# Attention's third score chunk directly behind the other two, in the projection banks; the slot projection in the first chunk's bank

## The reference

```python
def attn(x):                                  # 16 heads, 64 key dims, 64 slots, 128 value dims
    q, k, v = heads(x @ Wq), heads(x @ Wk), heads(x @ Wv)
    s = clip(heads(x @ Ws), -32, 32)          # slot scores
    z = cumlogsumexp(s, axis=time)
    g, p = exp(z_before - z), exp(s - z)
    # recurrence over time:  hk = hk * g + k p^T ;  ok = q . hk      (b h 64 slots)
    pv = softmax(ok)
    # recurrence over time:  hv = hv * g + p v^T ;  o = pv . hv
    o = o * rsqrt(mean(o^2) + EPS) * g_norm_weight * silu(x @ Wg)
    return o.reshape(...) @ Wo
x = layernorm(x + attn(x))
x = layernorm(x + cross_attention(q=x, k=ctx, v=ctx))   # 32 query heads over 8 key heads, 16 dims each
x = layernorm(x + ((silu((x @ gate_w.T) * gate_s) * ((x @ up_w.T) * up_s)) @ down_w.T) * down_s)
```

## Time and profile before

| | us |
|---|---|
| median of 3 runs | 2073.99 (2073.62 to 2078.05) |
| profiled execution | 2075.78 |
| its span | 2074.1 |
| TensorE busy | 2001.5 (97%) |
| VectorE busy | 1378.5 (66%) |
| ScalarE busy | 779.9 (38%) |
| GpSimd busy | 527.1 (25%) |
| mean granted clock of TensorE | 0.99 |

### The profile page before, as it was taken

How to read it: one execution, slowest core, us unless ns; L and a number is a source line. 1 busy time by engine, 2 the same in 40 slices (tenths; PEclk the granted TensorE clock), 3 DMA queues, 4 the chain that set the end, 5 groups by cost and what they waited for, 6 DMA issues and landing times. The chain is left out here.

```text
span 2074.1 us, 30680 instructions
## 1 busy us (share of the span) xinstructions
PE 2001.5 (97%) x11828; PEld 1436.9 (69%) x11828; DVE 1378.5 (66%) x2219; ACT 779.9 (38%) x1918; POOL 527.1 (25%) x575
## 2 busy tenths in 40 slices
PE   7999999999999999999999989999999799999997
PEld 6787877878778777787877753343433378787775
DVE  4666666566666666666666679999999265555556
ACT  2332232322323223232232326888888621211111
POOL 2142151141242143142241253222221011111111
PEclk9999999999999999999999998999999999999999
DMA  4000100001001001001000000111110100000002
GB/s 162 1 1 11 36 1 17 31 11 36 1 11 36 1 11 37 1 11 36 1 11 3 6 14 18 25 27 30 25 25 13 32 16 15 30 15 30 15 16 81
DMA packets 58609, 46.89 MB, mean 23 GB/s; under 512 B 14448, under 2 KB 47216, under 8 KB 58480
## 3 DMA queue, kind: packets, MB, share of 16 engines
q1 hardware_dynamic: 58480, 45.11, 7.3%
HBM read 32.78 MB, written 4.19 MB: 18 GB/s over the span
## 5 line engine op out<-in xcount | busy, mean ns | idle before, releaser
L1268 DVE TENSOR_REDUCE a_raw_qks<-a_ps 128x1 f32<-128x512 f32 x512 | 323.4, 684 | 20.8 <-PE a_ps L694 18.4
L1245 ACT ACTIVATE x_prob<-a_ps 128x512 f32<-128x512 f32 x512 | 279.3, 606 | 68.7 <-PE a_ps L716 67.7
L65 PE MATMUL a_ps<-a_vg_hi,a_xT_lo 128*128 128x512 f32 x512 | 209.6, 409 | 1.1 <-DVE a_vg_lo L1293 1.1
L66 PE MATMUL a_ps<-a_vg_lo,a_xT_hi 128*128 128x512 f32 x512 | 200.4, 391 | 0.0
L67 PE MATMUL a_ps<-a_vg_hi,a_xT_hi 128*128 128x512 f32 x512 | 199.9, 390 | 0.0
L65 PE MATMUL a_ps<-a_xT_hi,a_qks_lo 128*128 128x512 f32 x384 | 157.9, 411 | 1.9 <-DVE a_xT_lo L1299 1.9
L1320 DVE SCALAR_TENSOR_TENSOR a_gate<-a_gate,a_ps 128x256 f32<-128x256 f32 x128 | 52.0, 407 | 152.1 <-ACT a_gate L1136 152.1
L66 PE MATMUL a_ps<-a_xT_lo,a_qks_hi 128*128 128x512 f32 x384 | 150.7, 392 | 0.0
L67 PE MATMUL a_ps<-a_xT_hi,a_qks_hi 128*128 128x512 f32 x384 | 150.7, 392 | 0.0
L694 PE MATMUL a_ps<-a_xT_lo,a_xT_hi 64*128 64x512 f32 x384 | 144.7, 464 | 5.8 <-DVE a_raw_qks L1268 4.2
L579 POOL TENSOR_TENSOR a_f<-a_rs 128x8 f32<-128x8 f32 x32 | 6.5, 203 | 560.7 <-ACT a_flat L1164 560.7
(11 more groups left out here) (180 smaller groups left out, 4578.8 us busy)
## 6 DMA issues: line engine op xcount, KB each, us to landing
a_raw_vg<-in_L_attn_Wv_dram SPq DMA_DIRECT2D x8, 512.0 KB, 4.3
a_raw_vg<-in_L_attn_Wg_dram SPq DMA_DIRECT2D x8, 512.0 KB, 6.7
a_raw_qks<-in_L_attn_Wo_dram SPq DMA_DIRECT2D x8, 512.0 KB, 3.6
a_xT_lo<-a_xT_lo SPq DMA_DIRECT2D x32, 128.0 KB, 2.4
out_dram<-acc SPq DMA_DIRECT2D x8, 512.0 KB, 3.2
x_values<-acc SPq DMA_DIRECT2D x13, 256.0 KB, 2.7
acc<-in_x_dram SPq DMA_DIRECT2D x3, 1024.0 KB, 10.4
f_raw_down<-in_L_ffn_down_w_dram SPq DMA_DIRECT2D x11, 256.0 KB, 2.9
```

What stands on the lines that cost most here:

```text
L65: pe.matmul(out, w_lo, x_hi, start=start, stop=False)
L66: pe.matmul(out, w_hi, x_lo, start=False, stop=False)
L1245: nc.scalar.activation(prob[par][:, s % 4, :], score_bank(q, s, par), ACT.Exp, scale=X_SCALE).then_inc(exp_done[par], 1)
L1268: nc.vector.tensor_reduce(nm[:, q % 2, i % 4, par, i // 4:i // 4 + 1], max_bank(u, q, i, par), AX.X, ALU.max, negate=True).then_inc(max_re ...
```

## The change

In every step but the last, chunk 2 goes into the two projection banks, directly behind chunks 0 and 1, with no wait. S comes behind it, into `ch[0]` (for m > 0), and waits for ScalarE's copy of chunk 0 (`chunk_act` 2m - 1 = 2n + 1). VG follows S directly. It waits for VectorE to have masked head 0 of chunk 2, VG + 1 for head 1. In the last step chunk 2 stays in `ch` with its waits.

In the last step the diagonals go ahead of the first output tile, a second tile moves behind the values, and VectorE's split of the right operand goes ahead of `low_oT`; its additions move with the tiles. In the cross attention VectorE's `normalise` at s = 3 and s = 13 goes ahead of that slice's reductions.

```diff
--- before.py
+++ after.py
@@ -332,6 +332,14 @@
         EARLY = 6
         IN_VALUES = 10
 
+        def slot_bank(m, b):
+
+            return ch[0] if m else pj[b % 2]
+
+        def last_chunk_banks(n):
+
+            return ch if n == NSTEP - 1 else [pj[n % 2], pj[(n + 1) % 2]]
+
         def value_banks(n):
 
             return (okb, tb) if n == NSTEP - 1 else ob
@@ -760,16 +768,20 @@
 
             def project(m, i, b, pair):
 
-                bank = pj[(b + i) % 2]
+                bank = slot_bank(m, b) if i == S else pj[(b + i) % 2]
 
                 if i == S:
-                    wait(pe, right_ready, 2 * m - 1)
+                    wait(pe, chunk_act, 2 * m - 1)
                     pe.wait_ge(s_ready, pair + 1)
                 elif i == VG:
-                    wait(pe, left_ready, 2 * m - 1)
+                    if m:
+                        pe.wait_ge(chunk_dve, 4 * m - 1)
                     pe.wait_ge(vg_ready, pair + 1)
                 elif i == VG + 1:
-                    pe.wait_ge(clip_done, m + 1)
+                    if m:
+                        pe.wait_ge(chunk_dve, 4 * m)
+                    else:
+                        pe.wait_ge(clip_done, 1)
                 else:
                     pe.wait_ge(gate_ready, 4 * m + i - 2)
                 if i == Q:
@@ -809,10 +821,11 @@
 
             def last_chunk(n):
 
-                pe.wait_ge(chunk_act, 2 * n + 1)
-                pe.wait_ge(chunk_dve, 4 * n + 1)
+                if n == NSTEP - 1:
+                    pe.wait_ge(chunk_act, 2 * n + 1)
+                    pe.wait_ge(chunk_dve, 4 * n + 1)
                 for i, col, first in CHUNKS[2]:
-                    mm = blocks(ch, i, col, first, T)
+                    mm = blocks(last_chunk_banks(n), i, col, first, T)
                 mm.then_inc(chunk_done, 1)
 
             def diagonals(n):
@@ -894,9 +907,8 @@
                 pe.wait_ge(e_ready, n + 1)
                 into = n == NSTEP - 2
                 chunks(n)
-                next_project(S)
                 last_chunk(n)
-                next_project(VG)
+                next_project(S, VG)
                 slots(n)
                 states(n, j)
                 if not first:
@@ -975,14 +987,13 @@
                 transpose4(okb, [pv[:, 2 * t:2 * t + 2, :].rearrange("p h m -> p (h m)") for t in range(TT)])\
                     .then_inc(pvT_done, 1)
                 max_pair(0, 7)
-                project_out(n, PAIRS - 1, (0,))
                 pe.wait_ge(left_ready, 2 * n + 2)
                 pe.wait_ge(right_ready, 2 * n + 2)
                 diagonals(n)
-                project_out(n, PAIRS - 1, (1,))
+                project_out(n, PAIRS - 1, (0,))
                 max_pair(0, 8)
                 values(n, B - 1)
-                project_out(n, PAIRS - 1, (2, 3))
+                project_out(n, PAIRS - 1, (1, 2, 3))
                 for i in range(TILES):
                     max_pair(0, 9 + i)
                     if i > 1:
@@ -1312,7 +1323,7 @@
 
             def clip(m, b):
                 dve.wait_ge(proj_done, PROJ * m + 1)
-                nc.vector.tensor_scalar(eT[:, :], pj[b % 2], CLAMP, -CLAMP, ALU.min, ALU.max).then_inc(clip_done, 1)
+                nc.vector.tensor_scalar(eT[:, :], slot_bank(m, b), CLAMP, -CLAMP, ALU.min, ALU.max).then_inc(clip_done, 1)
 
             def gating(m, i, b):
 
@@ -1417,7 +1428,7 @@
                 norm_now = at(p, PAIRS - 1) and j > 0
                 into = n == NSTEP - 2
                 mask_chunks(n, ((0, 1, ch[1]), (1, 1, tb)))
-                mask_chunks(n, ((2, 0, ch[0]), (2, 1, ch[1])))
+                mask_chunks(n, ((2, 0, last_chunk_banks(n)[0]), (2, 1, last_chunk_banks(n)[1])))
                 low_left(eT[:, :], 2 * n + 1)
                 dve.wait_ge(left_ready, 2 * n + 2)
                 clip(n + 1, b1)
@@ -1480,14 +1491,14 @@
                 reduce_max(0, 0, 6)
                 slot_sum(n)
                 scaled_weights(n)
+                low_right(wT, 2 * n + 1)
                 low_oT(n)
-                low_right(wT, 2 * n + 1)
                 reduce_max(0, 0, 7)
                 mask_diagonal_blocks(n)
-                add_out(n, B - 2, (0, 1))
                 reduce_max(0, 0, 8)
+                add_out(n, B - 2, (0,))
                 gated_output(n, B - 1)
-                add_out(n, B - 2, (2, 3))
+                add_out(n, B - 2, (1, 2, 3))
                 for i in range(9, 14):
                     reduce_max(0, 0, i)
 
@@ -1531,11 +1542,13 @@
                                 dve.wait_ge(x_added, 2 * u)
                         if stats_unit and s == 14:
                             dve.wait_ge(norm.stats_ready, norm_of[2] + 1)
+                        if s == 3 and not (first and q == 0):
+                            normalise(u - 1, 1)
+                        if s == 13:
+                            normalise(u, 0)
                         for ahead, i in max_turns(first, q, s):
                             if not (last and q + ahead > 3):
                                 reduce_max(u + ahead, (q + ahead) % 4, i)
-                        if s == 3 and not (first and q == 0):
-                            normalise(u - 1, 1)
                         if s == 4 and not (first and q == 0):
                             add(u - 1, b if q else b - 1, (q - 1) % 4, 1)
                         if stats_unit and s in (6, 8, 10, 12):
@@ -1546,8 +1559,6 @@
                             dve.wait_ge(norm.done, TT * (B - 1))
                         if use_unit and s in (6, 8, 10, 12):
                             norm.apply(dve, *norm_of, tiles=[s // 2 - 3])
-                        if s == 13:
-                            normalise(u, 0)
                         if s == 14:
                             add(u, b, q, 0)
```

## The result

The changed kernel is slower by about 0.4%: 2082.75 us median against 2074.33 (8 runs each), a ratio of 1.0037 with a 95% interval of 1.0027 to 1.0048. The profiled execution took 2084.23 us, 8.45 more than the one before.

What follows compares the result with a forecast made beforehand. TensorE bounds the kernel, busy 594.72 of 594.87 us in the attention's steady steps, with VectorE close behind in the cross attention. Terms: 14.7 - 5.6 - 1.5 = +7.6 us, giving a 2081.6 us median; range 2076.5 to 2087.5.

Steps and rivals of the forecast that it cites:

- Part 1, the saved changes of shape: Attention steps, chunk 2 directly behind chunks 0 and 1: two changes of shape go, gaining 0.39 us a step, 31 steps.
- The rival that the bubbles belong to a new bank or to new weights: Attention steps: bubbles turn up behind chunk 2 again, no change of shape saved; +19.7 us, 2094 us; chance 0.04.
- Part 2, the stand: Attention steps: S waits for ScalarE's copy of chunk 0, TensorE stands 0.91 to 1.00 us; net 0.53 us slower a step.
- The 0.03 us that the first matmul was to save after a stand: Attention steps: the first matmul after a stand costs 0.03 us less than after a change of shape.
- the seven steps that start with the late begin: Attention: 7 of 30 steps begin 0.11 us later against ScalarE, held by VectorE's split; cost 0.42 us there.
- Part 3, the cross attention: Cross attention, normalisation ahead of the maxima: TensorE's transposes wait less, gaining 5.6 us, bounds 0 and 9.
- The 19 plain gaps: Cross attention: 19 places with 0.17 us hidden before the transposes; all go, 3.2 us.
- The 8 long ones: Cross attention: 8 visible TensorE waits for VectorE, 5.4 us in all; half kept as gain, 2.4 us.
- Part 4, the last step: Last attention step: diagonals start about 2 us earlier, values another 1 us or more; gain 1.5 us, bounds 0 and 3.
- S is not held: Attention steps: the copy's release reaches TensorE by 2.11 us, all 31 steps gain 0.39; -19 us, 2055 us; chance 0.07.
- The clock falls at the new stand: Attention steps: a 0.95 us stand drops TensorE's clock, 1.5 us or more a step; 2127 us or more; chance 0.02.

Runs made afterwards that it cites:

- the mended kernel: Changed kernel, but ScalarE copies chunk 0 of the next step between its fourth and fifth square; 2056.76 us, ratio 0.9908 to the kernel before.
- the ten squares: Two more ScalarE squares between the fourth and fifth of eight: in the changed kernel 2093.69 us, ratio 1.0082; in the kernel before, ratio 0.9996.

## Why the prediction was right

It gave 2081.6 us and the median is 2082.75. Its sum was +7.6 us; the difference of the medians is 8.4, and 7.7 by the ratio. The mechanism held, as the mended kernel and the ten squares show; that the number came so close is in part luck, since two errors cancelled. By its steps:

**Part 1, the saved changes of shape.** Forecast 0.39 us a step. The mended kernel, where nothing else is left, has 0.41 (37.18 to 36.77). Right. Before, the array's shape changed three times in this part of a step: from chunk 1 to S, from S to chunk 2 and from chunk 2 to VG. Two of the changes are gone, and the one that stays is from chunk 2 to S. The rival that the bubbles belong to a new bank or to new weights fell: chunk 2 now goes into two new banks with new weights, and its pairs still start at the plain pace. The runs put the price at about 0.2 us for each of the two changes, half of it in front of the first matmul of the new shape (0.32 and 0.21 us where 0.23 and 0.12 are plain) and half between that one and the next (0.22 and 0.34 where 0.12 and 0.23 are plain). The rule of the Trainium skill, "TensorEngine Tiling (Array Packing)", Key Properties, is that a change of mode drains TensorE. The runs agree with it, though they show only the bubbles and no drain as such.

**Part 2, the stand.** Forecast a start of S at 3.02 to 3.11 us and a stand of 0.91 to 1.00. S starts at 3.00, just under that, and it would have started at 2.09 (the mended kernel), so the stand is 0.91, the lower end. The release was dearer in the forecast than in the runs: 0.05 us for this releaser too, and the 128-row shape adds nothing, so the middle value of 0.10 was set too high. The 0.03 us that the first matmul was to save after a stand is not there (717.81 to 718.15 is 0.34). Net in a plain step 0.50 to 0.51, forecast 0.53. For the seven steps that start with the late begin I had 0.42; they grew by 0.33 (37.17 to 37.50), and S starts at 2.90 in them. Step 0 gained 0.47, forecast 0.39. Steps 0 to 29 together are +12.5, and with step 30 at +0.5 the sum is +13.0 where the forecast had +14.7, just under its own lower bound of 13.4 (13.5 with the stand of 0.91 put into its sum). The wait list was forecast with 25 to 29 us and has 24.4, since it leaves out the part of a stand that the modelled ends cover. That the stand is ScalarE's copy alone, and comes back in every step, is shown by the mended kernel and the ten squares.

**Part 3, the cross attention.** Forecast -5.6 with bounds 0 and -9; measured -5.8 in the trace and -4.4 (-6.2 to -2.5) by the ratio of the kernel with this edit alone. The division was right as well. The 19 plain gaps went entirely: their transposes start 0.32 to 0.33 us after the matmul before. The 8 long ones went too, but the maximum bank's wait has come in their place, so they gave about 2.5 us in all, where 2.4 was forecast.

**Part 4, the last step.** Forecast -1.5 with bounds 0 and -3. This was the weakest term. The diagonals do start almost 2 us earlier, as forecast, but the values only 2.1, where I had 2 and another 1 or more. I counted two tiles out of the way of the values. The second did leave, but the first took its place between the diagonals and the values, so only one tile went. And TensorE's stand was not shortened: 2.10 us for the right operand in place of 2.11 for the tile's low part. A tile that moves behind the values must still be done, so 0.8 us is left at the next maxima, and in the trace of this edit alone the clock took that too, to 0.04 at the first transpose. The ratio of that kernel can't tell 0 from 1.5 us.

**The rivals.** *S is not held* is the mended kernel: the price I gave it was -19 us. That kernel measured 2056.76 beside 2076.12, 19 us less, once the copy really ends before 2.11 us. *The clock falls at the new stand* didn't happen: the 602 us of steps 2 to 17 of the changed kernel have a granted clock of 1.00, with a stand of 0.9 us in each 37.6, and with the 1.2 us of the ten squares the 608 us of the same steps have 1.00 too. The Trainium skill, "TensorE: Matmul & The Clock Gate", The HAM clock gate, has the half clock as the default of an idle TensorE. The trace agrees in the last step, where the granted clock fell to 0.51 after a stretch with TensorE busy 0.99 of 3 us; a single stand of 0.9 us in an otherwise busy step did not bring it about.

**The luck in the total.** The terms as the traces have them are +13.0, -5.8 and about 0, together +7.2 beside the forecast's +7.6. The steps were forecast 1.7 us too dear, and the last step 1.5 us too good; the two nearly cancel. What is left to the measured 8.4 is no more than the clock at the turn of the stages moves by chance.

## What to carry to other kernels

When a step is moved forward on the bounding engine, look at the other engine's queue that frees its buffer, not at how long that engine's own piece takes: here a copy of 0.6 us stood behind 2 us of squares whose results nobody waited for so soon. In this way a regrouping that saves 0.4 us cost 0.5 net, and moving one copy on an engine with time to spare turned it into a gain of 0.4. So before such a move, bring the instruction that frees the buffer forward in its queue. A busy share of nearly 100% (594.72 of 594.87 us) doesn't mean that there is nothing to gain: the starts in order show gaps of 0.1 to 0.2 us that busy rows cover. And when a tile is moved out of the way, ask whether a stand goes with it: in the last step only the order changed, and the stand stayed as long as it was.

## What the runs showed of the hardware

- At the turn from the attention to the cross attention, where TensorE stands several times for 1 to 2 us, the same instructions after the same wait ran at 2.4 GHz in some traces and at 1.2 GHz in others: 16 matmuls in 2.05 or 3.52 us, 16 others in 2.37 or 3.83. This is worth 1.6 us in step 30 and 1.7 to 3 us in the stretch behind it. It is the likely reason for the spread of the times of the kernel before (2073.62 to 2078.05 us in the first three), which no run shows by itself; a gain of 1 us there can't be told from it.
- One stand of 0.9 us (1.2 with ten squares) in each 37.6 to 38.0 us of otherwise dense matmuls left the granted clock at 1.00 in all three traces that have it.
- From the recorded end of ScalarE's copy to the start of a 128-row matmul that waited for it: 0.05 us, about the 0.06 of a 64-row one.
- Two changes of the array's shape, from 64-row pairs to 128-row matmuls and back, cost 0.41 us a step together (37.18 to 36.77).
- A square of 128 columns on ScalarE takes 0.25 us from start to start with its sum (eight in 2.02 us) and 0.16 without (two in 0.32).
